# A different order for the opening of a fused feed-forward and attention kernel: full copies of x first, four chunk buffers, norms moved ahead of results, two chunks split by VectorE

## What is computed

```
xn = (x - mean) / sqrt(var + 1e-5)
routing   = softmax(xn @ gate_w.T)                    # 8 experts
in_scale  = routing @ in_channel_scale
out_scale = routing @ out_channel_scale
z   = (xn * in_scale) @ sign(weight).T * out_scale + bias
out = x + attention(xn, Wq, Wk, Wv, Wo) * silu(z)
```

## Time and profile before

| | |
|---|---|
| median of 3 runs | 1139.92 us |
| the profiled execution | 1140.27 us |
| its span | 1138.5 us |
| TensorE busy | 1107.5 us, 97% |
| VectorE, ScalarE, GpSimd busy | 70%, 56%, 34% |
| first matmul | 9.48 us |
| end of the first tile's matmuls | 43.74 us |
| first `in_scale` of round 1 | 74.44 us |
| transposes of tile 8 | 85.94 us |

### The profile page before, as it was taken

One profiled execution on the slowest core, in us unless ns is written; L12 is line 12 of the kernel. 1 busy time (PEld: TensorE's weight loads), 2 busy tenths in 40 slices (PEclk: granted clock), 3 DMA queues, 4 the chain that ended last, 5 costly groups with the idle time before them and its releaser, 6 DMA issues.

```text
span 1138.5 us, 17762 instructions
## 1 busy us (share of the span) xinstructions
PE 1107.5 (97%) x5620; PEld 925.2 (81%) x5620; DVE 798.3 (70%) x1860; ACT 639.6 (56%) x1344; POOL 385.2 (34%) x240
## 2 busy tenths in 40 slices
PE   4899999999999999999999999999999999999998
PEld 3667777888888888888888888888888887788887
DVE  6768641476767776767776677767677768899865
ACT  6545542366665666646566565666656667645341
POOL 0443646352342433334342352523424335200000
PEclk9899999999999999999999999999999999999999
DMA  9526133220202202021460202202022014586764
GB/s 368 209 93 241 55 94 111 75 65 11 64 9 74 64 10 64 9 64 49 172 221 9 64 18 64 64 9 64 9 74 64 10 64 168 188 282 219 235 212 148
DMA packets 88719, 116.40 MB, mean 102 GB/s; under 512 B 3440, under 2 KB 69104, under 8 KB 87664
## 3 DMA queue, kind: packets, MB, share of 16 engines
q1 hardware_dynamic: 88688, 116.01, 30.4%
HBM read 82.44 MB, written 33.55 MB: 102 GB/s over the span
## 4 chain that ended last, share of the span: by engine, by line
PE 87%; DVE 6%; ACT 3%; issue 1%; POOL 1%; DMA 1%; SPq 0%; DVEq 0%; POOLq 0%; ACTq 0%
PE at_proj L44 17%; PE at_proj L46 17%; PE at_proj L45 17%; PE at_out L1123 7%; PE at_pt L1110 6%; PE ff_z_ps L286 5%; PE at_score L1092 4%; PE at_score L1093 3%; POOL ff_xs_lo L669 1%; PE at_pt L44 1%; PE at_pt L46 1%; PE at_pt L45 1%; PE at_proj L1077 1%; PE at_score L44 1%; PE at_score L45 1%
## 5 line engine op out<-in xcount | busy, mean ns | idle before, releaser
L44 PE MATMUL at_proj<-xn_hi,w_hi 128*128 128x512 f32 x824 | 333.6, 405 | 1.6 <-POOL w_lo L1813 0.8
L46 PE MATMUL at_proj<-xn_hi,w_lo 128*128 128x512 f32 x824 | 322.8, 392 | 0.0
L45 PE MATMUL at_proj<-xn_lo,w_hi 128*128 128x512 f32 x824 | 321.3, 390 | 0.0
L46 PEld LDWEIGHTS at_proj<-xn_hi,w_lo 128*128 128x128 f32 x824 | 154.6, 188 | 34.5
L1797 POOL TENSOR_TENSOR at_turning<-at_turning,rope_table 128x512 f32<-128x512 f32 x64 | 82.8, 1294 | 289.4 <-DVE at_turning L1499 289.4
L44 PEld LDWEIGHTS at_proj<-xn_hi,w_hi 128*128 128x128 f32 x824 | 154.9, 188 | 29.1 <-issue 1.2
L45 PEld LDWEIGHTS at_proj<-xn_lo,w_hi 128*128 128x128 f32 x824 | 155.3, 188 | 27.5
L1297 ACT ACTIVATE at_prob<-at_score,at_neg_max 128x512 f32<-128x512 f32 (+3 forms) x256 | 133.5, 526 | 71.2 <-DVE at_neg_max L1527 70.8
L1805 POOL TENSOR_TENSOR w_lo<-w_stage,w_hi 128x1024 fp32r<-128x1024 f32 x45 | 114.4, 2558 | 162.9 <-ACT w_hi L1259 162.9
L1306 ACT ACTIVATE at_pt_hi<-at_pt 128x512 fp32r<-128x512 f32 (+1 forms) x192 | 94.0, 524 | 99.7 <-PE at_pt L1110 98.9
L1544 DVE TENSOR_TENSOR at_pt_lo<-at_pt,at_pt_hi 128x512 fp32r<-128x512 f32 (+1 forms) x192 | 112.1, 598 | 42.1 <-ACT at_pt_hi L1306 41.1
(11 more groups left out here) (214 smaller groups left out, 1924.9 us busy)
## 6 DMA issues: line engine op xcount, KB each, us to landing
w_stage<-_attn_hidden_states_dram SPq DMA_DIRECT2D x17, 512.0 KB, 6.4
z_store<-z SPq DMA_DIRECT2D x16, 512.0 KB, 2.8
w_stage<-in_L_attn_Wq_dram SPq DMA_DIRECT2D x16, 512.0 KB, 3.8
w_stage<-in_L_attn_Wk_dram SPq DMA_DIRECT2D x16, 512.0 KB, 5.1
w_stage<-in_L_attn_Wv_dram SPq DMA_DIRECT2D x16, 512.0 KB, 6.2
att_store<-at_att_t SPq DMA_DIRECT2D x32, 256.0 KB, 2.0
at_turning<-z_store SPq DMA_DIRECT2D x16, 512.0 KB, 5.4
w_stage<-in_L_attn_Wo_dram SPq DMA_DIRECT2D x12, 512.0 KB, 4.3
```

Of the source, the lines that this page charges most:

```text
L44: pe.matmul(out, sh, mh, start=first, stop=False, skip_group_check=reopened)
L45: pe.matmul(out, sh, ml, start=False, stop=False, skip_group_check=reopened)
L46: return pe.matmul(out, sl, mh, start=False, stop=final, skip_group_check=reopened)
```

## The change

In round 0 ScalarE makes only the full copy of each x tile ahead of the router (`x_copy`); the high and low parts, wanted only by the attention stage's store, are made later (`first_high`, `first_low`), from the full copy. In round 1 `x_low` reads `xn_full` instead of PSUM. Four buffers hold the chunks of round 0, two of them in `z`. Chunks 6 and 7 of round 0 are split on VectorE (`split_chunk`). The first tile's matmuls alternate the high part of chunk k with the low part of k-1 (`first_tile`). The matmuls of `warm` are 22, 6, 2, 7 and 2 instead of 6, 2 and 4, and 22 of them stand ahead of the first transposes. On TensorE the transposes, the router and the first `in_scale` of round 1 come one to three steps later in the order; on VectorE the norm of tiles 6 and 7 is finished ahead of `z_scale(1)`, and the norm of tiles 8 and 9 moves from ahead of the router of round 1 to behind `scale(1, range(4))`. The store of the first normalised batch moves behind `store_z(1)`.

```diff
-WARM = (6, 2, 4)
+WARM = (22, 6, 2, 7, 2)
...
+        def xs_buffer(r, k):
+
+            if r == 0 and k % 4 >= 2:
+                return z[:, 1, (k % 2) * SEQ:(k % 2 + 1) * SEQ]
+            return xs_full[:, k % 2, :]
...
+            def first_low(n):
+
+                tok = slice(n * P, (n + 1) * P)
+                if n >= 2:
+                    dve.wait_ge(first_hi, n - 1)
+                dve.tensor_tensor(xn[0][PLO][:, :, tok], xn_full[:, :, tok], raw(xn[0][PHI][:, :, tok]),
+                                  ALU.subtract).then_inc(first_lo, 1)
...
+                    whole = xn_full[:, ks, tok] if j == 1 else x_bank(n, b)
+                    dve.tensor_tensor(xn[j % 2][PLO][:, ks, tok], whole, raw(xn[j % 2][PHI][:, ks, tok]),
...
+            def split_chunk(k):
+
+                dve.wait_ge(scaled, k + 1)
+                dve.tensor_copy(xs_hi[:, k, :], xs_buffer(0, k)).then_inc(xs_dve_high, 1)
+                dve.wait_ge(xs_dve_high, k - ON_DVE + 1)
+                dve.tensor_tensor(xs_lo[:, k, :], xs_buffer(0, k), raw(xs_hi[:, k, :]), ALU.subtract).then_inc(xs_dve_low, 1)
...
             ln_finish(4, 2)
+            z_scale(0)
             ln_stats(6, 2)
-            z_scale(0)
-            for j in range(BATCH):
+            ln_finish(6, 2)
+            first_low(2)
+            z_scale(1)
+            first_low(3)
+            x_low(4)
+            x_low(5)
+            z_scale(2)
+            router(1)
+            scale(1, range(4))
+            x_low(6)
+            x_low(7)
+            ln_stats(8, 2)
+            z_scale(3)
+            for j in range(1, BATCH):
...
+                scale(j, range(4, KT))
+                if j == 1:
+                    ln_finish(m, 2)
```

More of the change, by code:

```diff
@@ L347, in _ @@
                     ffn(QT * j + 2, range(2, 5))
[L348 to L358, removed]
-                    if more:
-                        in_scale(j + 1, k - 4)
+                    if more:
+                        gate(j + 1)
+                    ffn(QT * j + 2, range(5, 7))
+                    if more:
+                        gate_transposes(j + 1)
+                    ffn(QT * j + 2, range(7, KT))
+                    ffn(QT * j + 3, range(4))
+                    if more:
+                        route_transposes(j + 1)
+                    for k in range(4, KT):
+                        ffn(QT * j + 3, (k,))
+                        if more:
+                            in_scale(j + 1, k - 4)
         @block.scalar
@@ L459, in _ @@
                 m = n + QT
[L460 to L463, removed]
+                out_scale(n, 0)
+                xs_high(j, range(4, KT))
+                out_scale(n, 1)
                 if not more:
@@ L612, in _ @@
             layer_norm(2)
-            x_low(1)
-            x_low(0)
-            x_low(2)
-            x_low(3)
             chan_low(0)
+            first_high(0)
+            first_low(0)
+            first_high(1)
             router(0)
@@ L636, in _ @@
                 m = n + QT
-                if j == 0:
+                scale(j, range(4, KT))
+                if j == 1:
+                    ln_finish(m, 2)
+                if more:
+                    ln_stats(m + 2, 2)
                     x_low(m)
+                z_scale(n)
+                if more:
                     ln_finish(m + 2, 2)
                     x_low(m + 1)
-                else:
-                    scale(j, range(4, KT))
-                    if more:
-                        ln_stats(m + 2, 2)
-                        x_low(m)
-                    z_scale(n)
-                    if more:
-                        ln_finish(m + 2, 2)
-                        x_low(m + 1)
                 z_scale(n + 1)
@@ L683, in _ @@
             pool.wait_ge(route_zero, 1)
-            xs_low(0, range(KT))
+            xs_low(0, range(ON_DVE))
             pool.wait_ge(bias_in, 16)
```

202 lines of the change are left out of this document (147 added, 55 removed).

## The result

The changed kernel takes 1147.5 us (median of 4 runs, 1146.75 to 1148.38), the kernel before, beside it on the same chip, 1139.81 us: ratio 1.0065, 95% interval 1.0048 to 1.0083. It is slower by 7.7 us; 1147.2 was forecast. Its profiled execution took 1148.38 us with a span of 1146.6; the profiled execution of before took 1140.27 us with 1138.5, so the two traces are 8.1 us apart.

The account below looks back on a forecast made before the run. TensorE, busy 97% of the span, was taken as the bound. 7.6 us gained, then 5.35 + 2.1 + 1.9 + 5.3 lost, put tile 8's transposes 6.95 later: 1140.27 + 6.95 = 1147.2 us; range 1136.5 to 1151.

Parts of the forecast that it names:

- The opening: Up to the first in_scale: earlier norm and fewer ScalarE copies bring it from 29.07 to 24.05 us; bounds -6.3 to -4.0.
- The chunks of round 0: First in_scale to first tile's end: ScalarE's queue becomes the limit; the tile ends at 37.7 us, 6.0 earlier.
- Tiles 1 to 3: TensorE's 30.1 us of work plus 1.85 of new waits put round 1's first in_scale at 68.7 us.
- Steps 1 and 2: Before scale(1,4) in round 1, only z_scale stood; now low parts of tiles 6 and 7 and statistics add 5.35 us.
- Step 3: Low parts of tiles 6 and 7 now read two SBUF inputs and lose turns to GpSimd: 2.1 us, bounds 0 to 2.1.
- Step 4: scale(1,4) is done at 83.0 us; in_scale(1,6) waits for it, so TensorE idles 8 us.
- Step 5: Norm of tile 8, its short operations losing turns to GpSimd, ends 9.9 us behind scale(1,4); bounds 5.8 and 9.9.
- rival C: TensorE's clock falls after the new idle stretch: up to 3.6 us past tile 8's transposes, 1149 to 1151; 0.17 with D.
- A: Between rounds 0 and 1 the shared port costs nothing; tile 8's transposes come 0.8 us later: 1141.1 us; chance 0.18.
- B: Opening gains exceed round-change losses, with GpSimd bounding the chunks and the port free: 3.8 us earlier, 1136.5; chance 0.17.
- D: New warm-up matmuls end at 11.5 us and delay the first transposes by two: 1149 us; chance 0.17 with rival C.
- Costed at nothing: First batch's store, moved behind store_z(1), was given no cost: its room is needed only more than 15 us later.

Follow-up runs that it names:

- e6_warm: Changed kernel with 6 instead of 22 warm-up matmuls ahead of the first transposes: 1150.69 us, ratio 1.0097.
- e9_twobuf: Changed kernel with the four chunk buffers of round 0 put back to two: 1149.54 us, ratio 1.0087.
- e2_xlow: Changed kernel with only the low parts of tiles 6 and 7 moved ahead of scale(1, range(4)) on VectorE: 1143.64 us, ratio 1.0036.
- e4_pool: Changed kernel with GpSimd made to wait for the norm of tile 8 ahead of z_bias(3): 1144.94 us, ratio 1.0047.
- e3_norm: Changed kernel with only the norm of tiles 8 and 9 moved back ahead of z_scale(2): 1141.29 us, ratio 1.0017.
- e1_both: Changed kernel with low parts of tiles 6 and 7 ahead of scale(1, range(4)) and norm of tiles 8 and 9 ahead of z_scale(2): 1136.19 us, ratio 0.9971.
- e8_clock: Changed kernel with 30 and 13 unread matmuls filling TensorE's two long waits of round 1: 1147.01 us, ratio 1.0066.
- e5_zscale: Kernel of e1_both with z_scale(1) moved ahead of the finish of the norm of tiles 6 and 7: 1137.75 us, ratio 0.9988.
- e10_gaps: Changed kernel with VectorE waiting for its own result after each of the eight low parts of tiles 4 to 7: 1147.17 us, one run.

## Why the prediction was right, step by step

**The opening.** First `in_scale` forecast at 24.05, measured 24.39; the last copy at 17.7, measured 17.97. The 22 matmuls end at 10.1, not 9: the first transposes start 0.5 us later than in e6_warm. I priced the warm-up as "no cost"; what I did not write down is that the rest of the opening's sum took the higher clock for granted, which is worth 3.1 us (e6_warm).

**The chunks of round 0.** The first tile's end at 37.7, measured 37.95. The order was as described: ScalarE's sixth high part at 34.16 (forecast 33.9), then VectorE's four operations, delayed by the port, then two half steps. (The forecast's terms add up to 33.7 and then 37.2, where it has 33.9 and 36.9; this is small.) Not foreseen was what the buffers do: I had them remove `scale`'s wait for GpSimd, which is true, but their 2.1 us arise at VectorE's last operations (e9_twobuf).

**Tiles 1 to 3.** The new wait of 1.45 us is there with 1.54 at 54.21; T is 69.37 against 68.7. But 68.7 is not the sum of its terms: 37.7, 30.1 and 1.85 make 69.65, and the 0.95 us taken off as "rounding" has no reason in any row. The terms were good to 0.3 us; the figure carried on was 0.7 too early.

**Round 0 to round 1.** Steps 1 and 2 hold. Step 3: 2.1 us was taken for the port, the four low parts show 1.84 over e2_xlow's 2.49. (One of the rows that it leans on does not show what is said of it: L559 at 89.78 began when GpSimd's addition, done at 89.84, was ending. The rows for a PSUM input beside GpSimd are L606 at 79.54 and L591 at 84.75, with 1.22 and 0.69, their usual times.) Step 4: the wait of `in_scale(1,6)` ends at 83.49 (83.0) after 7.3 us (8). Step 5: the norm of tile 8 came 9.45 behind that instead of 9.9, with its turns lost in the three operations named (the "seven" short operations are five; its 1.8 us is right for five). X: 92.9 forecast, 92.94 measured. That it is so close is luck: T was 0.7 later than forecast, the chain from T to X 0.7 shorter, and they cancel. From its own terms, with T at 69.65, the forecast would have been 93.9 for X and 1148.2 us. e4_pool and e2_xlow each take away one term of the sum, and X moves by that term (2.1 and 4.3); e3_norm takes away the waits for the norm, and X moves by 4.4 instead of 7.7, the rest being the clock. So the order and the port are shown as the cause, not only argued.

**What the sum left out.** The traces are 8.1 us apart where X is 7.0. About half of the rest is rival C, in small, and by another way than it says: the low stretch behind the 7.31 us was over before X, and a second one followed the wait of 3.41 us for the norm. I had given it up to 3.6 us; 1.6 stand at tile 9 and 0.6 at tile 10, where before had a wait of its own (0.84) that absorbs a part, and 0.5 at the first `in_scale` of round 2. Another 0.6 arises behind 124 us (at 1063 us the lag is 8.0); no run shows why. The profiled execution is the slowest of the four, and the forecast lay 0.3 us under their median.

**The rivals.** A (the port costs nothing) is refuted by e4_pool and by 4.33 against 2.49. B (the opening wins more) needed T below 67.9 and a free port. Neither held. It names the right neighbour, though: with both moves undone the rest of the change does win, 3.1 us. D did not come either: the 22 matmuls end at 10.1, not 11.5; they delay the first transposes by 0.5 us, and give back six times that. "Costed at nothing" held for the store: it goes out at 61.50, and nothing waits for it.

## What to carry to other kernels

A change of several parts is worth its parts one by one: here all but two moves together win (e1_both, 0.9971), and these two, in the first hand-over between rounds, cost 11 us. Work that is put ahead of a producer for which the bounding engine waits costs its full length, plus what it loses to the shared port, plus, in some executions, the lower clock behind the idle stretch (about 1 us in e8_clock's runs, 2.8 ahead of X in e3_norm's trace); so look whether the idle stretch ends straight at dense work. And of short two-input operations ask what GpSimd does at that moment: where its additions start decides more than the order of VectorE's own work (e4_pool, e5_zscale).

## What was not expected of the hardware

- Turns at the port are not simply alternate, as I had read from the two rows at 952 us. Five VectorE operations back to back held off a waiting GpSimd addition to their end (5.71 us instead of 2.4); a gap let it in (e10_gaps). At 74.44, where VectorE's first operation found GpSimd at work, GpSimd's two low parts took 2.98 instead of 2.53 and VectorE's four 4.33. Why VectorE's stream did not hold the port there is open. The Trainium skill, "SBUF — State Buffer", section "SBUF: two separate sides", says that of GpSimd's operations and VectorE's with two SBUF inputs or in a two-port mode, the one that begins first holds the shared pair of ports for its whole instruction and the other blocks. The trace agrees where one wait stands alone (L639 ended with `z_bias`, after 2.27 us).
- An operation on 128x2 elements waits as long as one on 128x512: 0.16 to 0.17 us became 0.69, 1.21, 2.27 and 2.39. RECIPROCAL at 87.42, with GpSimd at a low part since 87.00, took its usual 0.16.
- The length of a wait alone does not tell whether the clock falls. Two waits of 0.56 and 1.15 us were followed by the lower level in e1_both, and by 1.00 up to 79 us in the changed kernel; a wait of 1.88 us ahead of X by 0.50 in e8_clock, one of 2.36 us by 1.00 in e10_gaps. What decides between them is open.
